# Two-high row packing of the first expert products and of the last query projection in a hybrid conv-attention kernel

## The reference, cut to what matters

```python
def _moe(tokens, router_w, w1, b1, w2, b2):
    logits = tokens @ router_w.T
    probs = softmax(logits)                    # top 2 of 8 kept, renormalised -> combine
    ...
    for e in range(8):
        h = gelu(tokens @ w1[e] + b1[e], approximate=False)
        y = h @ w2[e] + b2[e]
        out = out + combine[:, e:e + 1] * y

def _L3_attn_ref(x, w_qkv, w_out, b_out):
    q, k, v = split(x @ w_qkv, 3)              # 64 -> 128 each
    k, v = inst_norm(k), inst_norm(v)          # per head of 16
    out = q @ (k.T @ v) / n                    # per head
    return out @ w_out + b_out
t = t + moe(layer_norm(t)); t = t + attn3(layer_norm(t))
```

## Time and profile before

| | |
|---|---|
| time, three runs | 988.42, 992.96, 993.91 us; median 992.96 us |
| profiled execution, first to last instruction (span) | 980.1 us |
| time of the profiled execution itself | not listed; the median is 12.9 us above the span |
| PE busy | 875.3 us, 89% of the span |
| DVE, ACT, POOL busy | 595.7, 457.1, 204.5 us |
| mean granted TensorE clock | 0.962 |
| chain that ended last, by engine | PE 58%, DVE 17%, ACT 11%, issue 6%, DMA 5% |

### The profile page before, as it was taken

The page is one execution under the profiler, slowest core; times in us unless marked ns, Lnnn a source line. Parts: engine busy times, 40 slices in busy tenths (PEclk is TensorE's granted clock), DMA queues, the critical chain, the costliest instruction groups (busy, mean ns, idle before and its releaser), DMA issues.

```text
span 980.1 us, 22296 instructions
## 1 busy us (share of the span) xinstructions
PE 875.3 (89%) x9216; PEld 588.9 (60%) x9216; DVE 595.7 (61%) x1666; ACT 457.1 (47%) x764; POOL 204.5 (21%) x274
## 2 busy tenths in 40 slices
PE   9888798999999999999999999999988879978876
PEld 8675475566666665666566566656555555644553
DVE  5545534673688468845884588558844764653456
ACT  1003326453555355525543655356435645524754
POOL 1002100120225012401341124112411231131122
PEclk9999689999999999999999999999979999998988
DMA  7100000000000000000000001000100100030000
GB/s 198 25 7 1 1 6 23 23 23 28 23 23 23 28 23 23 23 28 23 23 23 28 7 23 39 23 1 23 39 11 26 36 23 23 23 81 23 2 1 22
DMA packets 25572, 25.84 MB, mean 26 GB/s; under 512 B 14688, under 2 KB 20576, under 8 KB 25344
## 3 DMA queue, kind: packets, MB, share of 16 engines
q1 hardware_dynamic: 25472, 24.42, 8.7%
HBM read 19.69 MB, written 4.72 MB: 25 GB/s over the span
## 4 chain that ended last, share of the span: by engine, by line
PE 58%; DVE 17%; ACT 11%; issue 6%; DMA 5%; POOL 2%; SPq 1%; POOLq 0%; DVEq 0%; ACTq 0%
PE ring L934 7%; PE pv L955 5%; PE side_a L633 5%; PE ring L889 5%; PE pv L973 4%; ACT pr L1190 4%; DVE rden L1676 3%; DMA scale<-branch_scale 3%; PE heads L879 2%; PE side_a L642 2%; PE heads L914 2%; PE ring L929 2%; DMA branch_scale<-rden 2%; PE heads L861 2%; PE ring L897 2%
## 5 line engine op out<-in xcount | busy, mean ns | idle before, releaser
L1190 ACT ACTIVATE pr<-ring 128x1024 f32<-128x1024 f32 (+1 forms) x128 | 120.9, 944 | 108.3 <-PE ring L938 61.0
L934 PE MATMUL ring<-kq 64*128 64x256 f32 (+2 forms) x1280 | 136.5, 341 | 0.7 <-ACT kq L1242 0.5
L934 PEld LDWEIGHTS ring<-kq 64*128 64x128 f32 x1280 | 96.3, 191 | 42.6 <-issue 30.8
L1234 ACT ACTIVATE kq<-ring 128x896 f32<-128x896 f32 x64 | 58.8, 919 | 85.3 <-PE ring L889 85.3
L1686 DVE SCALAR_TENSOR_TENSOR ob<-pv,all_gates,scale 128x256 f32<-128x256 f32 x96 | 46.3, 482 | 85.3 <-PE pv L973 38.4
L1661 DVE TENSOR_REDUCE toks<-heads 128x2 f32<-128x512 f32 x64 | 44.3, 692 | 84.8 <-PE heads L919 83.4
L573 POOL TENSOR_TENSOR toks<-ta,tb 128x128 f32<-128x128 f32 (+1 forms) x96 | 39.7, 434 | 180.4 <-DVE tb L1652 180.4
L1242 ACT ACTIVATE kq<-ring 128x256 f32<-128x256 f32 x64 | 24.6, 384 | 107.5 <-PE ring L897 107.0
L1676 DVE RECIPROCAL rden<-pv 128x256 f32<-128x256 f32 x32 | 56.2, 1756 | 25.5 <-PE pv L955 25.0
L536 POOL TENSOR_TENSOR oT<-ob 128x256 f32<-128x256 f32 x32 | 23.3, 727 | 226.3 <-DVE ob L1686 226.3
L889 PE MATMUL ring<-early,toks 128*128 128x128 f32 x448 | 63.5, 284 | 7.5 <-ACT pr L1190 7.4
(11 more groups left out here) (377 smaller groups left out, 1704.4 us busy)
## 6 DMA issues: line engine op xcount, KB each, us to landing
scale<-branch_scale SPq DMA_DIRECT2D x128, 96.0 KB, 2.3
branch_scale<-rden SPq DMA_DIRECT2D x32, 128.0 KB, 1.7
late<-in_late SPq DMA_DIRECT2D x1, 2158.5 KB, 8.4
xin<-in_x SPq DMA_DIRECT2D x16, 64.0 KB, 2.2
pr<-in_prep SPq DMA_DIRECT2D x1, 602.0 KB, 3.8
y<-ob SPq DMA_DIRECT2D x8, 64.0 KB, 1.9
kq<-in_masks SPq DMA_DIRECT2D x1, 480.0 KB, 8.5
toks<-in_final SPq DMA_DIRECT2D x1, 434.0 KB, 4.4
```

The source lines that it names most:

```text
L934: m = pe.matmul(ring[:, j, at:at + nq], kq[rows, k, key0:key0 + P], kq[rows, k, Q + q_:Q + q_ + nq], start=r % 2 == 0, stop=at > P)
L1190: act.activation(out, in_, ACT.Exp, scale=SCALE).then_inc(S("exp_done"), 1)
L1234: act.activation(kq[:, k, :], flat[:, 0:WIDE], ACT.Copy).then_inc(S("turned"), 1)
```

## The change

The normalised tokens for the first mixture and the second attention are written twice side by side (128 tokens x 2 copies x 64 channels), turned in one 128x128 transpose each, and copied to all 128 rows of `xpT`, so that rows 64 to 127 hold the tokens again. Two more DMAs put tiles 2 and 3 of `w1` and the weights of `q3` on rows 64 to 127. The four first expert products come together behind the wait for `logit_exp`, in two pairs: one of each pair contracts over rows 0 to 63 into SC, the other over rows 64 to 127 into SB_. The `q3` product is put on rows 64 to 127 between the two `kv3` products, which use rows 0 to 63. ACT waits once for `hidden`. The addition of the normalised tokens to the residual (DVE L1537) reads one of the two copies.

```diff
--- before.py
+++ after.py
@@ -180,7 +180,7 @@
         cnH = sb("cnH", [P, T])
         xnH = sb("xnH", [P, T])
         selH = sb("selH", [P, KEEP])
-        xp = sb("xp", [P, NT, C])
+        xp = sb("xp", [P, NT, 2, C])
         xpT = sb("xpT", [P, T])
         sbc = ktok
         ranks = sb("ranks", [P, NT])
@@ -447,6 +447,9 @@
             a, v = lo["w_v1"][0], lo["w_v"][0]
             sp.dma_start(late[96:P, a:a + HEADS * VDIM], late_in[32:C, a:a + HEADS * VDIM]).then_inc(S("head_weights"), 16)
             sp.dma_start(late[C:P, v:v + HEADS * VDIM], late_in[0:C, v:v + HEADS * VDIM]).then_inc(S("head_weights"), 16)
+            a, q = lo["w1"][0] + 2 * P, lo["q3"][0]
+            sp.dma_start(late[C:P, a:a + 2 * P], late_in[0:C, a:a + 2 * P]).then_inc(S("head_weights"), 16)
+            sp.dma_start(late[C:P, q:q + P], late_in[0:C, q:q + P]).then_inc(S("head_weights"), 16)
             for x in range(2):
                 sp.dma_start(w_vs[C * x:C * x + C, :], late_in[C:P, v + T * x:v + T * x + T])\
                     .then_inc(S("head_weights"), 16)
@@ -597,6 +600,13 @@
                     m = pe.transpose(dst[0:C, col + t * P:col + (t + 1) * P], src[:, t, :], ident)
                 m.then_inc(S(done), 1)
 
+            def turn_twice(done):
+
+                pe.sem_inc(S("pe_gap"), 1)
+                for t in range(NT):
+                    m = pe.transpose(SB_[:, t * P:(t + 1) * P], xp[:, t, :, :].rearrange("p x c -> p (x c)"), ident)
+                m.then_inc(S(done), 1)
+
             IDLE = dict(loads=24, route1=4, route2=12,
                         gn1_done=(0, 10), kv1_copied=(4, 4), kv_ready=(2, 2), kv_masked=(1, 0), o0_ready=(8, 6),
                         gn2_stats=(4, 1), gn2_done=(9, 2), x2=(1, 0), xn1=(8, 4), xnT1=(1, 0), small_copied=(1, 0),
@@ -742,20 +752,20 @@
                 yield
                 busy(4, SB_)
                 after(n, "xn2")
-                transpose_tok(xp, SB_, 0, "xn2_turned")
+                turn_twice("xn2_turned")
                 yield
                 after(n, "xnT2")
                 for t in range(NT):
                     m = pe.matmul(SB_[:, t * E:(t + 1) * E], xpT[:, t * P:(t + 1) * P], cst("r2"),
                                   start=True, stop=True)
                 m.then_inc(S("logits"), 1)
-                for i in range(2):
-                    m = pe.matmul(SC[:, i * T:(i + 1) * T], w1[:, i, :], xpT[:, :], start=True, stop=True)
-                m.then_inc(S("hidden"), 1)
                 yield
                 pe.wait_ge(S("logit_exp"), image * 2 + 2)
                 for i in range(2):
-                    m = pe.matmul(SB_[:, i * T:(i + 1) * T], w1[:, 2 + i, :], xpT[:, :], start=True, stop=True)
+                    for x in range(2):
+                        rows = slice(C * x, C * x + C)
+                        m = pe.matmul((SC, SB_)[x][:, i * T:(i + 1) * T], w1[rows, 2 * x + i, :], xpT[rows, :],
+                                      start=True, stop=True)
                 m.then_inc(S("hidden"), 1)
                 yield
                 after(n, "gelu1")
@@ -766,13 +776,15 @@
                     m.then_inc(S("expert_out"), 1)
                 yield
                 after(n, "xn3")
-                transpose_tok(xp, SB_, 0, "xn3_turned")
+                turn_twice("xn3_turned")
                 yield
                 after(n, "xnT3")
-                pe.matmul(SC[:, 0:T], cst("q3"), xpT[:, :], start=True, stop=True).then_inc(S("q3_out"), 1)
-                for t in range(NT):
-                    m = pe.matmul(SB_[:, t * T:(t + 1) * T], xpT[:, t * P:(t + 1) * P], cst("kv3"),
+                for t in range(NT):
+                    m = pe.matmul(SB_[:, t * T:(t + 1) * T], xpT[0:C, t * P:(t + 1) * P], cst("kv3")[0:C, :],
                                   start=True, stop=True)
+                    if t == 0:
+                        pe.matmul(SC[:, 0:T], cst("q3")[C:P, :], xpT[C:P, :], start=True, stop=True)\
+                            .then_inc(S("q3_out"), 1)
                 m.then_inc(S("kv3_out"), 1)
                 yield
                 after(n, "kv3_normed", "q3_copied")
@@ -835,7 +847,7 @@
                 if kind is None and users is heads_users:
                     pe.wait_ge(S("tables_kept"), 1)
                     pe.wait_ge(S("tok_set"), 3)
-                    pe.wait_ge(S("head_weights"), 16 * 28)
+                    pe.wait_ge(S("head_weights"), 16 * 30)
                 if kind == "S":
                     pe.wait_ge(S("exp_done"), n * PARTS + k + 1)
                 if kind == "T":
@@ -1149,22 +1161,22 @@
                 yield
             def back(n, image):
                 after(n, "xn2_turned")
-                act.activation(xpT[0:C, :], SB_[0:C, 0:T], ACT.Copy).then_inc(S("xnT2"), 1)
+                act.activation(xpT[:, :], SB_[:, 0:T], ACT.Copy).then_inc(S("xnT2"), 1)
                 yield
                 after(n, "logit_max")
                 for t in range(NT):
                     act.activation(pe8[:, t, :], SB_[:, t * E:(t + 1) * E], ACT.Exp, bias=c8[:, t, 1:2],
                                    accum_out=c8[:, t, 2:3]).then_inc(S("logit_exp"), 1)
                 yield
+                act.wait_ge(S("hidden"), image + 1)
                 for u in range(2):
-                    act.wait_ge(S("hidden"), image * 2 + u + 1)
                     for i in range(2):
                         a = act.activation(hm[:, 2 * u + i, :], (SC, SB_)[u][:, i * T:(i + 1) * T], ACT.Gelu,
                                            bias=cst("b1")[:, 2 * u + i:2 * u + i + 1])
                 a.then_inc(S("gelu1"), 1)
                 yield
                 after(n, "xn3_turned")
-                act.activation(xpT[0:C, :], SB_[0:C, 0:T], ACT.Copy).then_inc(S("xnT3"), 1)
+                act.activation(xpT[:, :], SB_[:, 0:T], ACT.Copy).then_inc(S("xnT3"), 1)
                 yield
                 after(n, "q3_out")
                 act.activation(q3[:, :], SC[:, 0:T], ACT.Copy).then_inc(S("q3_copied"), 1)
@@ -1410,8 +1422,10 @@
             def layer_apply(n, t, mv_, gv_, out, which):
                 after(n, f"ln{which}_rstd")
                 for i in range(NT):
-                    a = V.tensor_scalar(out[:, i, :], t[:, i, :], mv_[:, i, 0:1], gv_[:, i:i + 1],
-                                        ALU.subtract, ALU.mult)
+                    from_ = t[:, i, :]
+                    if which in (2, 3):
+                        from_ = from_.unsqueeze(1).broadcast_to((P, 2, C))
+                    a = V.tensor_scalar(out[:, i], from_, mv_[:, i, 0:1], gv_[:, i:i + 1], ALU.subtract, ALU.mult)
                 if which < 5:
                     a.then_inc(S(f"xn{which}"), 1)
                 else:
@@ -1534,7 +1548,7 @@
                 link(V.tensor_reduce(c8[:, :, 0], SB_[:, 0:NT * E].rearrange("p (t e) -> p t e", t=NT),
                                      AX.X, ALU.max))
                 V.tensor_scalar(c8[:, :, 1], c8[:, :, 0], -1.0, None, ALU.mult).then_inc(S("logit_max"), 1)
-                V.tensor_tensor(t2[:, :, :], t2[:, :, :], xp[:, :, :], ALU.add)
+                V.tensor_tensor(t2[:, :, :], t2[:, :, :], xp[:, :, 0, :], ALU.add)
                 yield
                 dve.wait_ge(S("logit_exp"), image * 2 + 2)
                 link(V.reciprocal(c8[:, :, 3], c8[:, :, 2]))
```

## The result

The changed kernel takes 988.52 us (median of 20 runs, 983.66 to 997.54), the kernel before 986.71 us in 20 runs of the same comparison: a ratio of 1.0058, 95% interval 1.0034 to 1.0082. I had forecast 0.1% faster. The ratio leaves out every run more than 1.5% above the fastest of its kernel, and since the kernel before has one run of 972.13 us, that takes ten of its twenty runs and none of the changed kernel's. So the half percent in this ratio is too large. The plain means of the same runs are 989.2 and 986.0 us, 3.2 us apart with a standard error of 1.4. The plain means over all runs whose clock is on record (32 of the changed kernel, 99 later ones of the kernel before) are 988.6 and 986.6 us: 0.2% slower, 2.0 us with a standard error of 0.9. The change does not gain; the loss is small and known to about half its own size.

A forecast was written before the change was run, and what follows sets the result against it. PE is busy 89% of the span, but ACT and DVE set the pace at both changed places. Image terms -0.84 - 0.24 + 0.22 + 0.10 - 0.23 = -1.0 us, off the median: 992.0 us, range 986.5 to 997.0.

The forecast's parts named there:

- rival B: Before the scores PE waits 0.6 us more, with less array work; one more half-clock stretch gives 998.7 us; chance 0.09.
- My argument against B: From 240 to 480 us the clock was full throughout at 93% PE busy, with waits of this size in it.
- The door in front of the scores: Images 0 to 5: even scores wait for ACT's ring copy, so only 0.29 us of 0.94 can be had.
- My bound of 0.05 us for a change between row modes: New row-half groups: scores on row halves take 0.96 us, the same array time on full rows 0.91.
- ACT's cover: Second half of the hidden product: ACT's table load and GELUs set the pace, leaving PE 0.87 us to spare.
- Transposes and writes: Twice per image: wider transposes taken at 0.09 us, doubled DVE writes at 0.065 us each, partly covered.
- The projections: Second attention: 0.45 us less PE work per image, but DVE's maxima let 0.08 us through in images 0, 2, 3.
- The sum of the path: All images together: -1.0 us of the 9.3 us that PE saves, with bounds from -2.6 to 0.
- Rival A: PE is the bound after all: the whole 9.3 us comes through, giving 983.7 us; chance 0.11.
- rival C: Pairs don't overlap: hidden products behind the scores take 1.85 us instead of 0.91, projections win nothing, 993.4 us; chance 0.05.
- The base: Starting time: median of three runs, 12.9 us above the profiled span of 980.1 us; the difference was taken off it.

The follow-up runs named there:

- the kernel with that gap alone: Changed kernel with the projections put back on full rows, keeping doubled tokens and paired hidden products: median 986.91 us, ratio 0.9985.
- the dummies at m3: Four dummy products of 128 columns before PE's wait for m3, images 0 to 6: median 976.31 us on the changed kernel, 980.13 on the kernel before.
- the two sets: The changed kernel's first 20 runs, median 988.52 us, and its repeat without edit, median 988.21 us; at equal clock 986.8 and 985.3 us.
- the unpaired version: Changed kernel with the q3 product on rows 0 to 63 like the kv3 products, so the three no longer overlap: median 986.42 us, ratio 0.9997.

## Why the prediction was wrong

- **The step that failed** is the clock, which my sum left out: I took the clock of one profile for the kernel's and gave a shift only as rival B, with a chance of 0.09. It is the cause of the loss: -0.0044 of mean clock, 3.4 us. B's reason ("PE waits some 0.6 us more in front of the scores") and its place were wrong too: the kernel with that gap alone has its clock at 0.9570. Its second reason, less array work, is not enough by itself either: 0.9572 without the q3 product. Of B only the direction came true. Most falls of the steady state sit behind the wait for m3, where I had seen one (714 us) and did not ask what filled the other images' waits; the change adds some behind the packed projections. My argument against B, that from 240 to 480 us waits of this size went without a fall, came from one execution; over nine profiles seven in ten of the long waits at m3 had one. B's price was a single fall of 6.7 us in every run; what came is worth half of one per run.
- **The door in front of the scores**: right. The scores start 0.26 us nearer to the transposes (forecast 0.1 to 0.2), after a wait of 0.45 us for L1254 (forecast some 0.6).
- **What I called covered or small around it**: the scores' own group, started from a standstill, takes 1.06 us instead of 0.96, and the hidden group between full-row groups 1.07 instead of 0.96; the second lies under ACT's cover, as forecast. My bound of 0.05 us for a change between row modes was read from a group that follows L872, itself on 64 rows; in the same profile L934 takes 1.07 us wherever it follows L973, which contracts over all rows. From the transposes to the end of the scores' group the place gives -0.16 us, with the longer write about -0.1; forecast -0.14.
- **Transposes and writes**: both below my middle values. L607 to the next group takes 0.34 us against 0.31, +0.03 where I took 0.09. A doubled write takes 342 ns in the median against 308, +0.034 us where I took 0.065: the 256-element row that gave my slope is a poor neighbour. The doubled tokens cost 1.2 us in all at an equal clock (forecast 1.4) and come out 0.7 us shorter with the dummies at m3, so the sum of their cost is not measured.
- **The projections**: wrong size. I let 0.08 us per image through because DVE's maxima hold L879. The projections' group shrank by 0.34 us, and in image 0 L891 starts 6.77 us behind the projections against 6.97: 0.20 us come through. 0.08 of it is the slack in front of L879, as forecast. The rest is DVE's own chain, which I held fixed: its maxima L1676 start 6.03 us behind the projections instead of 6.15. At an equal clock the packed projections are 2.8 us under the doubled tokens alone without the dummies at m3 and 0.3 with them, where I had forecast 0.7; the total stays open.
- **The sum of the path**: forecast -1.0 us with bounds 0 and -2.6 (my terms give -2.4 for the lower one), measured -1.3 at an equal clock, -0.8 and -2.3 in the two sets. That this lies at the forecast is partly luck: the errors went in both directions, the parts don't add, and the full-clock periods of images 0 and 3 shrank by 0.56 and 0.35 us where I had 0.22.
- **Rival A** (all of PE's 9.3 us) is refuted, **rival C** (no overlap) too: pairs start 0.01 us apart, and the hidden group takes 1.07 us instead of 1.8.
- **The base**: the profiled execution of before had a clock of 0.962 and its own time was about 982 us (in the other runs of this kernel time and span differ by 1.7 to 1.9 us), not 12.9 us above its span. The three runs shown first have a median 6.3 us above that of all twenty (986.71). By the line a clock lower by 0.008 would do that, but theirs is not on record. So the forecast time of 992.0 us started from a base 6.3 us too high; that the measured 988.5 us lies in my range of 986.5 to 997.0 is luck.

**What stays open** is why the packed projections bring more falls. With them the clock is 0.9504 to 0.9519 in two kernels (44 runs), without them or with dummies ahead of them 0.9560 to 0.9572 in five. Missing work alone doesn't do it, and the unpaired version lies between. The profiles show additional falls directly behind the projections, but too few to account for the whole loss. With the dummies at m3, some 20 us later, the clocks of the two kernels no longer differ that way (0.9664 and 0.9651), and how those dummies could act on the place behind the projections is not shown.

## What to carry to other kernels

Before costing an edit in a kernel with one core and a high PE share, look for the places where the granted clock falls, and over several executions: a few dummy products in front of one wait brought 6.7 us here, although they lengthen the path, while the change without them lost 2.0 us and with them gains 2.8. Time taken off PE is worth having only if the gap that it leaves, or that it widens later on, doesn't bring the lower clock. When the effect is below one per cent, lay runs out as time against mean clock: most of the scatter is then the clock. What is left at an equal clock is known to 1 or 2 us here, not to the 0.3 us of its statistical error, so check it against image periods at full clock in the traces.

## What the runs showed of the hardware that I had not expected

- Between 260 and 840 us the clock falls though PE is never idle for more than 2.4 us at a time: at waits of 0.95 to 2.4 us for m3, in 22 of 31 cases (17 of 22 with one-column products in front, 5 of 9 without). Four products of 128 columns in place of 1 us of such a wait removed the falls (0 of 30). A wait of 1.35 us right behind 1.16 us of such products had none in 36 cases.
- Behind a fall the lower level can last 13 us with PE busy throughout (521 to 534 us above), so that a wait of 1.11 us costs 5 us.
- The Trainium skill (TensorE: Matmul & The Clock Gate, HAM oscillation) describes falls behind long idle gaps between bursts; here a single wait of 0.95 to 2.4 us was enough in 22 of 31 cases.
- A group of four 64-row products takes 1.07 us behind a group with another number of rows and 0.96 us behind a 64-row group. The Trainium skill (TensorEngine Tiling (Array Packing), Key Properties) says that a change of tiling mode drains the engine. The trace fits that with 0.1 us as the size, but does not single it out: behind a 64-row group and a wait of 0.45 us (L946 in image 0), without a change of mode, the group takes the same 0.1 us more.
